# Attention with residual and layer norm over 32 batches: orders of their own for the first two and the last three batches

## The chip, the cores and the metric

The kernel runs on one NeuronCore of a Trainium2 chip. Its engines are TensorE (PE), VectorE (DVE), ScalarE (ACT), GpSimd (POOL) and SyncE (SP), which only issues DMAs here. The metric is the device time of one execution in microseconds (us), lower is better.

## The reference

For each of 32 batches: x is 256 rows of 384, adj is a 256 x 256 bias. Twelve heads of 32.

```python
q = (x @ Wq.T).reshape(B, N, 12, 32); k = (x @ Wk.T)...; v = (x @ Wv.T + bv)...
a = jnp.einsum('bnhd,bmhd->bhnm', q, k) * 384 ** -0.5 + adj[:, None]
pad_mask = jnp.all(a == 0, axis=-1)                    # such a row gives zero
a = nan_to_num(softmax(where(pad_mask[..., None], -inf, a)))
o = jnp.einsum('bhnm,bmhd->bnhd', a, v).reshape(B, N, 384) @ Wo.T + bo
out = layernorm(x + o)                                 # eps 1e-5, no scale
```

## The kernel before

Every engine has one program written out by hand, and only semaphores tie them together. A product in full precision is made of three: each operand is split into a high part (a rounding copy) and a low part (the difference), and PE multiplies high by high, high by low and low by high (`product`, line 534).

**Names.** The 384 columns are three groups of 128 (four heads each). `project_kq(t, name)` makes two of the six pieces of k and q of batch t: K01 in `bank_c`, K2Q0 and Q12 in `bank_b`, 18 products of 256 columns each. `save_kq` (ACT) copies the bank to `kq`, `split_kq` (POOL) makes `kq_hi` and `kq_lo`. `project_v(t, c)` makes half of v (9 products of 384 columns), `save_v` (DVE) adds the bias. `scores(t, g)` makes the scores of group g, 24 small products into the four banks `s_bank`. A unit u (0 to 11, four per group) is two heads for one half of the rows. `add_bias(t, u)` (DVE, line 784) adds adj and finds the maximum, `exps(t, u)` (ACT, line 439) takes the exponentials into `prob`, a ring of four.

**Two ways to turn the probabilities.** Groups 0 and 1: `square` (DVE, line 798) turns 32 x 32 squares into a staging area that lies in `w_f`, where the weights were loaded. When the four squares of a group stand, SP issues `store_squares` (to HBM) and, when that has landed, `load_squares` (back, blocks in the right partitions), each 1 MB. Group 2: `transposes` on PE into `bank_t`, `copy_probT` on ACT. Then `weigh(t, g)` (line 621) multiplies by v into `bank_a`, and `save_o` (ACT) copies.

**The end of a batch.** `invert` (DVE) and `widen_inv` (POOL) make the inverse sums, `spread` (PE, line 602) turns them into `bank_c`, `divide` (DVE) applies them; `split_o_hi` is ACT's, `split_o_lo` POOL's (line 346). `project_y(t, c)` multiplies by the output weights into `bank_b`; `residual` (DVE, line 872) adds x, to which POOL has added the bias (`add_bo`, which waits for the load `xr<-in_x`); `moments` (DVE), `deviation` (POOL), `normalise` (ACT), `store_out` (SP). `find_zero`, `flag` (PE, line 628), `read_flag` and `mask` (DVE) test once per batch whether a row of scores can be all zero; `mask` loads a register and branches over work that is not done here.

**Order.** Each engine has a function `step(t)` in which calls for batches t+2, t+1, t, t-1 and t-2 stand in a fixed order. `steps` runs it for t from -3 to 33, and calls for batches that don't exist are skipped (`alive`). So the first and the last batches run in the same order as the middle, with holes. Before a bank is written again PE waits until its reader is done (for instance `kq_saved`, `v_saved`, `y_saved` for `bank_b`). Before the first step, SP issues the loads of x, of k's weights in three pieces and of q's in one, and PE runs 24 warm-up products of 256 columns (`keep_warm`).

Of the kernel before, what the change touches and what calls it, by code (L numbers as in the profile page):

```python
# [3 lines left out]
F32 = mybir.dt.float32  # L4
# [3 lines left out]
ALU = mybir.AluOpType  # L8
# [5 lines left out]
P = 128  # L14
# [13 lines left out]
PROB_RING = 4  # L28
WARM_START = 24
DMA = 16  # L30
# [19 lines left out]
class Batch:  # L50


    def __init__(self, c):
        self.c, self.p = c, c % 2
        self.alive = 0 <= c < B
        self.first = c == 0
# [21 lines left out]


def steps(body):  # L80
    for c in range(-3, 34):
        body(Batch(c))


def build(nc, x, xT, adj, adjP, wqT, wkT, wvT, bv, woT, bo, out):
# [66 lines left out]

    W_Q, W_K, W_V, W_O = range(4)
    W_SPLIT = {W_Q: KC + 1, W_V: KC + 2, W_O: KC + 3}
# [3 lines left out]
    w_loaded = {w: sem(f"w_loaded_{name}") for w, name in ((W_Q, "q"), (W_V, "v"), (W_O, "o"))}  # L158
# [56 lines left out]
    with nc.Block() as block:  # L215

        @block.sync
        def _(sp):
# [38 lines left out]
            def store_out(t):  # L257
                sp.wait_ge(y_ready, t.count(NT, NT))
                sp.dma_start(out[t.c].rearrange("(c p) d -> p c d", p=P), y_out[:]).then_inc(stored, DMA)
# [10 lines left out]
            load_w(W_Q, wqT)  # L270
            load_bias_sq(Batch(0))
            load_xt(Batch(1))
            load_w(W_V, wvT)
            load_b(bv_all, bv)
            load_bias(Batch(0))
            load_b(bo_all, bo)
            load_w(W_O, woT)

            def step(t):
# [4 lines left out]
                if nxt.alive and not nxt.first:  # L284
                    load_bias(nxt)
                if t.alive:
                    store_squares(t, 0)
                if nxt3.alive and nxt3.c >= 2:
                    load_xt(nxt3)
                if t.alive:  # L290
                    load_squares(t, 0)
                    store_squares(t, 1)
                    load_xr(t)
                    load_squares(t, 1)
                if nxt2.alive and not nxt2.first:
                    load_bias_sq(nxt2)
                if prev2.alive:
                    store_out(prev2)

            steps(step)  # L300
            sp.wait_ge(stored, DMA * B)

        @block.gpsimd
        def _(pool):
# [69 lines left out]

            def step(t):
# [4 lines left out]
                if prev.alive:  # L380
                    widen_inv(prev)
                if nxt2.alive and not nxt2.first:
                    split_xt(nxt2)
                if nxt.alive:
                    split_kq(nxt, "K2Q0")
                    split_kq(nxt, "Q12")
                    split_kq(nxt, "K01")
# [578 lines left out]
```

## Time and profile before

| what | us |
|---|---|
| median of 3 runs | 763.73 |
| lowest and highest | 762.37 and 765.3 |
| the profiled execution | 762.95 |
| its span, first to last instruction | 761.0 |

The profiled execution took 1.95 us more than its span. All 22949 instructions are written out, none is looped. The mean granted clock of TensorE over the span is 0.978. Times in the rows below count from the start of the span.

### The profile page before, as it was taken

The numbers are of one execution on the slowest core, as the hardware profiler recorded it, in microseconds if no ns is written. First come the engines' busy times: TensorE is split into PE (matmuls) and PEld (weight loads), VectorE is DVE, ScalarE is ACT, GpSimd is POOL, SyncE is SP. The second block draws the span as 40 slices with busy tenths as digits, with TensorE's granted clock in tenths as the row PEclk, the third lists the DMA queues.
The fourth block names the chain that finished last, engine by engine and source line by source line (L and its number), as shares of the span: only waits on it lengthen the run. The fifth ranks groups of instructions, "written<-read, shape, count | busy, mean of one in ns | idle before, by whom it ended". The sixth has DMA issues, their size and how long they took to land.

```text
span 761.0 us, 22949 instructions
## 1 busy us (share of the span) xinstructions
PE 716.0 (94%) x7480; PEld 609.5 (80%) x7480; DVE 587.8 (77%) x2216; ACT 615.5 (81%) x1991; POOL 453.1 (60%) x518
## 2 busy tenths in 40 slices
PE   6889999999999999999999999999999999998753
PEld 5777888888888888888888888888888888886532
DVE  2677788888888888888888888888888888788821
ACT  2678888888988898888888988888889889888721
POOL 3345676766666676666666766666667666665331
PEclk7999999999999999999999999999999999999985
DMA  8087788888877877878778788777887887777631
GB/s 260 3 284 243 265 286 278 271 283 274 275 262 258 284 243 282 299 273 285 263 258 283 239 286 286 253 261 275 300 285 238 287 281 246 283 275 257 234 102 43
DMA packets 92664, 193.00 MB, mean 254 GB/s; under 512 B 4736, under 2 KB 51584, under 8 KB 84352
## 3 DMA queue, kind: packets, MB, share of 16 engines
q1 hardware_dynamic: 92544, 191.52, 74.7%
q8 instruction: 61, 1.00, 0.5%
q14 instruction: 59, 0.48, 0.2%
HBM read 111.80 MB, written 79.69 MB: 252 GB/s over the span
## 4 chain that ended last, share of the span: by engine, by line
PE 87%; DMA 3%; DVE 3%; POOL 2%; issue 2%; ACT 2%; SPq 0%; ACTq 0%; POOLq 0%; DVEq 0%
PE bank_b L534 45%; PE bank_a L621 12%; PE s_bank L580 11%; PE bank_t L591 9%; PE bank_c L534 9%; PE bank_c L602 2%; DVE neg L784 1%; DMA w_f<-in_wqT 1%; DMA xr<-in_x 1%; DMA sq_probT<-sq_dram 1%; POOL o_lo L346 1%; POOL kq_lo L336 1%; DMA sq_dram<-w_f 1%; ACT prob L439 1%; DVE w_f L798 0%
## 5 line engine op out<-in xcount | busy, mean ns | idle before, releaser
L439 ACT ACTIVATE prob<-neg,negmax 128x256 f32<-128x256 f32 x768 | 380.7, 501 | 40.8 <-DVE negmax L784 38.3
L784 DVE CUSTOM_DVE_ANT_0 neg<-s_bank,bias_sq 128x256 f32<-128x256 f32 x512 | 190.9, 410 | 48.9 <-PE s_bank L580 44.0
L798 DVE STREAM_TRANSPOSE w_f<-prob 128x512 f32<-128x512 f32 x256 | 173.1, 695 | 0.0
L439 ACT ACTIVATION_READ_ACCUMULATOR prob<-neg,negmax 128x1 f32 x768 | 147.9, 193 | 0.0
L336 POOL TENSOR_TENSOR kq_lo<-kq,kq_hi 128x512 fp32r<-128x512 f32 x96 | 124.2, 1293 | 7.7
L534 PE MATMUL bank_b<-xt_hi,w_hi 128*128 128x256 f32 x384 | 116.8, 304 | 7.1 <-DVE w_lo L760 3.3
L534 PE MATMUL bank_b<-xt_lo,w_hi 128*128 128x256 f32 x384 | 109.8, 286 | 0.0
L534 PE MATMUL bank_b<-xt_hi,w_lo 128*128 128x256 f32 x384 | 109.5, 285 | 0.0
L362 POOL TENSOR_SCALAR var_eps<-meanvar 128x2 f32<-128x2 f32 x32 | 7.3, 228 | 168.1 <-DVE meanvar L882 168.1
L784 DVE CUSTOM_DVE_ANT_0 neg<-s_bank,bias 128x256 f32<-128x256 f32 x256 | 92.3, 416 | 10.5 <-PE s_bank L580 10.5
L372 POOL TENSOR_TENSOR xr<-xr,bo_all 128x768 f32<-128x768 f32 x32 | 59.2, 1849 | 53.2 <-DMA xr<-in_x 53.1
L534 PEld LDWEIGHTS bank_b<-xt_hi,w_hi 128*128 128x128 f32 x384 | 74.3, 193 | 16.5 <-DVE w_lo L765 2.6
L591 PE MATMUL bank_t<-ident,prob 128*128 128x128 f32 x512 | 83.3, 285 | 2.2 <-ACT probT L449 2.1
L872 DVE TENSOR_TENSOR y<-bank_b,xr 128x384 f32<-128x384 f32 x64 | 35.7, 558 | 60.5 <-PE bank_b L534 60.3
L591 PEld LDWEIGHTS bank_t<-ident,prob 128*128 128x128 f32 x512 | 53.9, 141 | 33.1 <-issue 26.1
L534 PE MATMUL bank_b<-w_hi,o_hi 128*128 128x384 f32 x192 | 70.0, 365 | 10.7 <-POOL o_lo L346 9.8
L346 POOL TENSOR_TENSOR o_lo<-o_n,o_hi 128x512 fp32r<-128x512 f32 x64 | 63.9, 1020 | 24.8 <-ACT o_hi L464 24.7
L449 ACT ACTIVATE probT<-bank_t 128x512 f32<-128x512 f32 x128 | 75.0, 586 | 1.0 <-PE bank_t L591 1.0
L534 PEld LDWEIGHTS bank_b<-xt_lo,w_hi 128*128 128x128 f32 x384 | 74.8, 195 | 0.0
L534 PEld LDWEIGHTS bank_b<-xt_hi,w_lo 128*128 128x128 f32 x384 | 74.8, 195 | 0.0
L621 PE MATMUL bank_a<-sq_probT,v 128*32 128x256 f32 x1024 | 68.9, 386 | 2.5 <-DMA sq_probT<-sq_dram 2.4
L534 PE MATMUL bank_b<-w_hi,xt_hi 128*128 128x384 f32 x192 | 70.2, 366 | 0.7 <-ACT kq L422 0.7
(66 smaller groups left out, 1793.9 us busy)
## 6 DMA issues: line engine op xcount, KB each, us to landing
sq_dram<-w_f SPq DMA_DIRECT2D x64, 1024.0 KB, 6.4
sq_probT<-sq_dram SPq DMA_DIRECT2D x64, 1024.0 KB, 6.2
xt<-in_xT SPq DMA_DIRECT2D x32, 384.0 KB, 5.7
xr<-in_x SPq DMA_DIRECT2D x32, 384.0 KB, 6.1
out_y<-y_out SPq DMA_DIRECT2D x32, 384.0 KB, 6.4
bias_sq<-in_adjP SPq DMA_DIRECT2D x32, 256.0 KB, 6.4
bias<-in_adj SPq DMA_DIRECT2D x32, 256.0 KB, 6.9
w_f<-in_wkT SPq DMA_DIRECT2D x3, 192.0 KB, 4.3
```

Source lines behind the costliest of these rows:

```text
L336: nc.gpsimd.tensor_tensor(kq_lo[t.p][:, a:a + 2, :], kq[:, a:a + 2, :], kq_hi[t.p][:, a:a + 2, :].bitcast(F32), ALU.subtract).then_inc(kq_ ...
L346: nc.gpsimd.tensor_tensor(o_lo[:, a:b], o_n[:, a:b], o_hi[:, a:b].bitcast(F32), ALU.subtract).then_inc(o_ready, 1)
L372: nc.gpsimd.tensor_tensor(xr[t.p][:], xr[t.p][:], bo_all[:].unsqueeze(1).to_broadcast([P, NT, D]), ALU.add).then_inc(xr_ready, 1)
L439: nc.scalar.activation(prob[:, u % PROB_RING, k], neg[:, h, w.c], ACT.Exp, scale=-1.0, bias=negmax[t.p][:, w.c, h:h + 1], accum_out=sums[t ...
L449: nc.scalar.activation(probT[:, a:a + PAIR, :, P * w.c:P * (w.c + 1)], bank_t[:], ACT.Copy).then_inc(probT_act, 1)
L534: last = nc.tensor.matmul(ps, w_pair[a](k), m_pair[b](k), start=(k == 0 and e == 0), stop=(k == KC - 1 and e == 2))
L580: last = nc.tensor.matmul(s_bank[j][:, c, :], a[t.p][rows, KC + g, P * c:P * (c + 1)], b[t.p][rows, g, :], start=(e == 0), stop=(e == 2))
L591: last = nc.tensor.transpose(bank_t[:, k, m, :], prob[:, u % PROB_RING, k, P * m:P * (m + 1)], ident[:])
L621: last = nc.tensor.matmul(bank[f"PV{g}"][HD * j:HD * (j + 1), 0:N], v[t.p][:, m, HD * h:HD * (h + 1)], weights, start=(m == 0), stop=(m == ...
L784: nc.vector.tensor_tensor_reduce(out=neg[:, h, w.c], in0=s_bank[h % JH][:, w.c, :], in1=by[t.p][:, w.c, :], scale=-1.0, scalar=BIG, op0=AL ...
L798: nc.vector.transpose(sq_stage[w.g][:, :, a:a + PAIR, :, w.c].rearrange("p b h m s -> p (h m) b s"), prob[:, u % PROB_RING].rearrange("p k ...
L872: nc.vector.tensor_tensor(y[:, c, :], bank[f"Y{c}"][:, 0:D], xr[t.p][:, c, :], ALU.add).then_inc(y_saved, 1)
```

## The change

`steps` and `alive` are gone. Each engine has now three parts: `start()`, which covers what the old steps -3 to 1 did; `step(t)` for t from 2 to 28, word for word the old order; and `end()`, which covers the old steps 29 to 33. In `start` and `end` the calls stand in another order, written out for each engine. Further:

- q's weights are loaded, and split on ACT and DVE, in three pieces, as k's are.
- `scores` waits for K01 and K2Q0 with group 0 and for Q12 with group 1 only.
- For batch 31, spread, project_y, and weigh of groups 1 and 2 use banks of the scores and `bank_c` instead of the shared ones; before, these waited for the readers of the shared banks, and now for all of DVE's reductions.
- The low part of o of batch 31 is made on DVE.
- The last output is stored in two halves.
- The 24 warm-up products are of 128 columns; none are put between the first pieces (`FIRST_WARM` is 0, 0, 0).
- `w_hi` and `w_lo` of v and of the output weights move to other places in ACT's and DVE's lists, and squares of batch 0 wait for them, as they overwrite `w_f`.

```diff
-    W_SPLIT = {W_Q: KC + 1, W_V: KC + 2, W_O: KC + 3}
+    W_SPLIT = {W_K: 0, W_Q: KC, W_V: 2 * KC + 1, W_O: 2 * KC + 2}
...
+    last_bank = {"R0": s_flat[0], "Y0": s_flat[0], "R1": s_flat[1], "Y1": s_flat[1], "PV1": s_flat[2], "PV2": bank_c[:]}
+    def bank_at(t, name):
+        return last_bank[name] if t.last and name in last_bank else bank[name][:]
...
-            load_w(W_Q, wqT)
+            for k in range(KC):
+                sp.dma_start(w_f[:, W_Q, k], wqT[P * k:P * (k + 1), :]).then_inc(wq_loaded[k], DMA)
+            load_xt(Batch(1))
             load_bias_sq(Batch(0))
-            load_xt(Batch(1))
             load_w(W_V, wvT)
...
             def scores(t, g):
                 if g == 0:
                     pe.wait_ge(kq_ready["K01"], t.count(1, 1))
                     pe.wait_ge(kq_ready["K2Q0"], t.count(1, 1))
+                if g == 1:
                     pe.wait_ge(kq_ready["Q12"], t.count(1, 1))
...
         @block.tensor
...
+            def start():
...
+                project_kq(t0, "K01")
+                project_kq(t0, "K2Q0")
+                pe.wait_ge(kq_saved["K2Q0"], t0.count(1, 1))
+                project_kq(t0, "Q12")
+                scores(t0, 0)
+                pe.wait_ge(kq_saved["Q12"], t0.count(1, 1))
+                project_v(t0, 0)
+                pe.wait_ge(kq_saved["K01"], t0.count(1, 1))
+                project_kq(t1, "K01")
+                scores(t0, 1)
...
         @block.tensor
...
+            def end():
...
+                project_y(t30, 0)
+                copied(t31, 10)
+                transposes(t31, 11)
+                pe.wait_ge(neg_ready, t31.count(H * NT, H * NT))
+                weigh(t31, 1)
+                pe.wait_ge(neg_ready, t31.count(H * NT, H * NT))
+                spread(t31, 0)
+                pe.wait_ge(y_saved, t30.count(NT, 1))
+                project_y(t30, 1)
+                pe.wait_ge(o_n_ready, t30.count(2, 2))
+                weigh(t31, 2)
+                pe.wait_ge(neg_ready, t31.count(H * NT, H * NT))
+                spread(t31, 1)
+                pe.wait_ge(o_n_ready, t31.count(2, 1))
+                project_y(t31, 0)
+                pe.wait_ge(o_n_ready, t31.count(2, 2))
+                project_y(t31, 1)
...
         @block.gpsimd
...
+            def end():
...
+                add_bo(t29)
+                add_bo(t30)
+                split_o_lo(t30, 0)
+                split_o_lo(t30, 1)
+                deviation(t29)
+                widen_inv(t31)
+                add_bo(t31)
+                deviation(t30)
+                deviation(t31)
...
         @block.sync
...
+            def end():
...
+                store_squares(t31, 0)
+                store_out(t27)
+                load_squares(t31, 0)
+                store_squares(t31, 1)
+                store_out(t28)
+                load_squares(t31, 1)
+                load_xr(t31)
+                store_out(t29)
+                store_out(t30)
+                store_out(t31)
```

**Where instructions move.** First POOL at the start, from its first split on. Here `kq_hi0<-kq` is the split of a piece of batch 0, told apart by the semaphore it waits for, and `xt_hi1<-xt1` the split of x of batch 1. Before:

```order
L323 CAST xt_hi1<-xt1 128x768 [waits xt_ready,xt_loaded1]
L325 TENSOR_TENSOR xt_lo1<-xt1,xt_hi1 128x768 [waits xt_hi_ready]
L334 CAST kq_hi0<-kq 128x512 [waits kq_saved_K2Q0]
L336 TENSOR_TENSOR kq_lo0<-kq,kq_hi0 128x512 [waits kq_hi_ready_K2Q0]
L334 CAST kq_hi0<-kq 128x512 [waits kq_saved_Q12]
L336 TENSOR_TENSOR kq_lo0<-kq,kq_hi0 128x512 [waits kq_hi_ready_Q12]
L334 CAST kq_hi0<-kq 128x512 [waits kq_saved_K01]
L336 TENSOR_TENSOR kq_lo0<-kq,kq_hi0 128x512 [waits kq_hi_ready_K01]
```

and in the changed kernel:

```order
L398 CAST kq_hi0<-kq 128x512 [waits kq_saved_K01]
L400 TENSOR_TENSOR kq_lo0<-kq,kq_hi0 128x512 [waits kq_hi_ready_K01]
L398 CAST kq_hi0<-kq 128x512 [waits kq_saved_K2Q0]
L400 TENSOR_TENSOR kq_lo0<-kq,kq_hi0 128x512 [waits kq_hi_ready_K2Q0]
L387 CAST xt_hi1<-xt1 128x768 [waits xt_ready,xt_loaded1]
L389 TENSOR_TENSOR xt_lo1<-xt1,xt_hi1 128x768 [waits xt_hi_ready]
L398 CAST kq_hi0<-kq 128x512 [waits kq_saved_Q12]
L400 TENSOR_TENSOR kq_lo0<-kq,kq_hi0 128x512 [waits kq_hi_ready_Q12]
```

K01 moved from third to first, and x of batch 1 now stands behind K2Q0.

Second, DVE's last instructions, from the last reciprocal (`inv<-sums1`, batch 31) on. `y<-bank_b,xr0` is a residual of batch 30, `y<-...,xr1` of batch 31, `o_n` a division. Before:

```order
L853 RECIPROCAL inv<-sums1 128x24 [waits inv_wide_ready,prob_ready]
L872 TENSOR_TENSOR y<-bank_b,xr0 128x384 [waits y_ready,xr_ready,y_done]
L877 BN_STATS stats<-y 128x6 [waits y_saved]
L882 BN_AGGR meanvar<-stats 128x2 [waits bn_ready,rstd_ready]
L872 TENSOR_TENSOR y<-bank_b,xr0 128x384 [waits xr_ready,y_done]
L877 BN_STATS stats<-y 128x6 [waits y_saved]
L882 BN_AGGR meanvar<-stats 128x2 [waits bn_ready]
L862 TENSOR_TENSOR o_n<-o_raw1,bank_c 128x512 [waits o_ready,inv_spread,o_saved1,o_saved0]
L862 TENSOR_TENSOR o_n<-o_raw1,bank_c 128x256 [waits inv_spread,o_ready,o_saved2]
L872 TENSOR_TENSOR y<-bank_b,xr1 128x384 [waits y_ready,xr_ready,y_done]
```

and in the changed kernel:

```order
L1255 RECIPROCAL inv<-sums1 128x24 [waits inv_wide_ready,prob_ready]
L1283 TENSOR_TENSOR y<-bank_b,xr0 128x384 [waits y_ready,xr_ready,y_done]
L1288 BN_STATS stats<-y 128x6 [waits y_saved]
L1293 BN_AGGR meanvar<-stats 128x2 [waits bn_ready,rstd_ready]
L1264 TENSOR_TENSOR o_n<-o_raw1,s_bank0 128x512 [waits o_ready,inv_spread,o_saved1,o_saved0]
L1283 TENSOR_TENSOR y<-bank_b,xr0 128x384 [waits xr_ready,y_done]
L1288 BN_STATS stats<-y 128x6 [waits y_saved]
L1293 BN_AGGR meanvar<-stats 128x2 [waits bn_ready]
L1264 TENSOR_TENSOR o_n<-o_raw1,s_bank1 128x256 [waits inv_spread,o_ready,o_saved2]
L1274 TENSOR_TENSOR o_lo<-o_n,o_hi 128x512 [waits o_hi_ready,y_done]
L1274 TENSOR_TENSOR o_lo<-o_n,o_hi 128x256 [waits o_hi_ready]
L1283 TENSOR_TENSOR y<-s_bank0,xr1 128x384 [waits y_ready,xr_ready,y_done]
```

The division of batch 31 stands between the two residuals of batch 30 and reads `s_bank0` and `s_bank1`; the two low parts are new on DVE.

Third, SP at the start: q's weights (`w_f<-in_wqT`) and what stands around them. Before:

```order
L223 DMA xt0<-in_xT 128x3x256
L269 DMA w_f<-in_wkT 128x384 x3
L262 DMA w_f<-in_wqT 128x3x384
L232 DMA bias_sq0<-in_adjP 128x2x256
L223 DMA xt1<-in_xT 128x3x256
L262 DMA w_f<-in_wvT 128x3x384
```

and in the changed kernel:

```order
L228 DMA xt0<-in_xT 128x3x256
L280 DMA w_f<-in_wkT 128x384 x3
L282 DMA w_f<-in_wqT 128x384 x3
L228 DMA xt1<-in_xT 128x3x256
L237 DMA bias_sq0<-in_adjP 128x2x256
L273 DMA w_f<-in_wvT 128x3x384
```

One load of 128 x 3 x 384 became three of 128 x 384, and x of batch 1 moved ahead of the bias.

## Rows read from the trace of the kernel before

**Rows 1.** The page's first part: busy us (share of the span) xinstructions.

```profile
PE 716.0 (94%) x7480; PEld 609.5 (80%) x7480; DVE 587.8 (77%) x2216; ACT 615.5 (81%) x1991; POOL 453.1 (60%) x518
```

**Rows 2.** Windows: stretch, length, busy by engine, PE's clock, DMA share, GB/s.

```profile
73.30:95.60 22.30, 22.07 (x238) 18.76 (x234) 18.38 (x70) 18.25 (x61) 14.38 (x17) 1.00 0.73 251
95.60:117.45 21.85, 21.85 (x238) 18.72 (x234) 18.07 (x70) 19.00 (x64) 14.98 (x17) 1.00 0.82 278
663.95:761.00 97.05, 67.34 (x634) 54.18 (x630) 56.46 (x204) 57.11 (x183) 39.12 (x52) 0.88 0.52 186
```

**Rows 3.** Groups by form in 109.3 to 131.2: busy us, mean ns | idle before.

```profile
L784 DVE CUSTOM_DVE_ANT_0 neg<-s_bank,bias_sq 128x256 f32<-128x256 f32 x16 | 6.0, 411 | 1.6 <-PE s_bank L580 1.6
L798 DVE STREAM_TRANSPOSE w_f<-prob 128x512 f32<-128x512 f32 x8 | 5.4, 696 | 0.0
```

**Rows 4.** Chain that ended last, 0 to 70: start us, us, what.

```profile
11.30 1.37 DVE w_lo L765
...
15.05 0.61 ACT kq L422
...
15.70 4.21 PE bank_b L534 x18
...
24.52 1.28 POOL kq_lo L336
...
25.84 0.98 PE s_bank L580 x24
26.82 2.35 PE bank_b L534 x18
...
38.02 4.71 DMA sq_dram<-w_f
...
42.82 5.94 DMA sq_probT<-sq_dram
```

**Rows 5.** Timeline of PE at 9.7: start us, us, instruction, [idle before].

```profile
9.74 0.39 PE L534 MATMUL bank_b<-xt_hi,w_hi 128*128 128x256 f32 x1 [1.92 <-DVE w_lo L760]
```

**Rows 6.** Windows of the fill; the clock is the third number from the end.

```profile
10.40:12.70 2.30, 0.00 (x0) 0.00 (x0) 1.36 (x1) 0.87 (x1) 0.67 (x1) 0.54 0.99 320
15.00:20.70 5.70, 5.01 (x24) 5.00 (x24) 0.00 (x0) 1.20 (x2) 2.14 (x3) 0.50 0.60 212
20.70:25.00 4.30, 3.98 (x33) 3.77 (x31) 0.35 (x1) 2.44 (x3) 3.00 (x4) 0.98 0.02 4
```

**Rows 7.** Timeline of DVE, 24 to 50.

```profile
24.65 2.35 DVE L765 SCALAR_TENSOR_TENSOR w_lo<-w_f,w_hi 128x1152 fp32r<-128x1152 f32 x1 [11.98 <-ACT w_hi L406]
...
32.21 1.35 DVE L765 SCALAR_TENSOR_TENSOR w_lo<-w_f,w_hi 128x1152 fp32r<-128x1152 f32 x1
...
46.41 0.42 DVE L784 CUSTOM_DVE_ANT_0 neg<-s_bank,bias_sq 128x256 f32<-128x256 f32 x1 [1.85 <-ACT prob L439]
```

**Rows 8.** Timeline of SP: issues of stores and loads of squares.

```profile
43.30 1.34 SPq L245 DMA_DIRECT2D sq_dram<-w_f  x1
...
51.35 0.36 SPq L254 DMA_DIRECT2D sq_probT<-sq_dram  x1
...
716.01 0.33 SPq L245 DMA_DIRECT2D sq_dram<-w_f  x1
...
725.47 0.36 SPq L254 DMA_DIRECT2D sq_probT<-sq_dram  x1
```

**Rows 9.** Chain that ended last, 690 to 761.

```profile
719.42 6.91 DMA xr<-in_x
...
733.53 1.41 PE bank_a L621 x16
...
737.05 1.80 PE bank_b L534 x9
...
750.15 3.26 PE bank_b L534 x9
...
753.44 0.57 DVE y L872
```

More of the change, by code:

```diff
@@ L379, in step @@
                 prev2 = t.later(-2)
[L380 to L387, printed above, removed]
-                if prev2.alive:
-                    deviation(prev2)
-                if t.alive:
-                    add_bo(t)
-                if prev.alive:
-                    split_o_lo(prev, 0)
-                    split_o_lo(prev, 1)
@@ L530, in _ @@
+            start()
+            for c in range(2, 29):
+                step(Batch(c))
+            end()
         @block.tensor
@@ L748, in _ @@
-            steps(step)
+                copied(prev, 10)
+                transposes(prev, 11)
+                pe.wait_ge(v_saved, t.count(NT, 1))
+                project_v(t, 1)
+                pe.wait_ge(o_n_ready, prev2.count(2, 2))
+                project_kq(nxt, "K01")
+                pe.wait_ge(v_saved, t.count(NT, 2))
+                project_y(prev2, 0)
+                pe.wait_ge(o_saved[0], prev.count(1, 1))
+                weigh(prev, 1)
+                scores(t, 2)
+                pe.wait_ge(y_saved, prev2.count(NT, 1))
@@ new lines, in step @@
+                project_kq(nxt2, "K2Q0")
+                pe.wait_ge(o_saved[1], prev.count(1, 1))
+                weigh(prev, 2)
+                copied(prev, 11)
+                transposes(t, 8)
+                pe.wait_ge(kq_saved["K2Q0"], nxt2.count(1, 1))
+                project_y(prev2, 1)
+                pe.wait_ge(kq_saved["K01"], nxt.count(1, 1))
+                spread(prev, 0)
+                pe.wait_ge(o_saved[2], prev.count(1, 1))
+                flag(t)
+                copied(t, 8)
@@ new lines, in step @@
+                transposes(t, 9)
+                scores(nxt, 0)
+                pe.wait_ge(y_saved, prev2.count(NT, 2))
+                project_kq(nxt2, "Q12")
+                pe.wait_ge(flag_read, t.count(1, 1))
+                weigh(t, 0)
+                copied(t, 9)
+                transposes(t, 10)
+                pe.wait_ge(o_n_ready, prev.count(2, 1))
+                spread(prev, 1)
+                pe.wait_ge(kq_saved["Q12"], nxt2.count(1, 1))
+                project_v(nxt, 0)
@@ L750, in _ @@
+            start()
+            for c in range(2, 29):
+                step(Batch(c))
+            end()
         @block.vector
@@ L935, in step @@
-                if prev.alive:
-                    divide(prev, 1)
-            steps(step)
+                add_bias(t, 3)
+                square(t, 0)
+                save_v(t, 0)
+                square(t, 1)
+                add_bias(t, 4)
+                square(t, 2)
+                add_bias(t, 5)
+                save_v(t, 1)
+                invert(prev)
+                add_bias(t, 6)
+                square(t, 3)
+                add_bias(t, 7)
+                residual(prev2, 0)
@@ L941 @@
+            start()
+            for c in range(2, 29):
+                step(Batch(c))
+            end()
 _INS = ["x", "xT", "adj", "adjP", "wqT", "wkT", "wvT", "bv", "woT", "bo"]
```

946 lines of the change are left out of this document (705 added, 241 removed).

## The prediction

> **What bounds the kernel now.** Read the page's line of engines first [rows 1]: TensorE (PE) is busy for 94% of the span. Then the windows cut where PE enters a step [rows 2]. A step of the middle takes 21.85 us and PE is busy for all of it, VectorE (DVE) for 18.07 and ScalarE (ACT) for 19.00. From PE's entry into step 3 (95.60) to that into step 29 (663.95) are 26 steps in 568.35 us, 21.86 each. So PE bounds the middle, and 32 batches at that pace are 699.2 us. The span is 761.0: 61.8 us lie in filling and draining. The stretch before step 2 ends at 73.30, and the one from step 29 is 97.05 long with PE busy for 67.34, part of that at half clock [rows 2]. The change rewrites these two stretches; the 27 steps between keep their order. So the sum has three terms: when PE enters step 2, the middle, and what follows PE's entry into step 29.
>
> **The middle.** Now 22.30 for step 2, then 568.35 [rows 2]. The finer waits of scores change nothing here: in a step K01 is the last of the three that POOL splits, before and after. Step 2's extra 0.45 is a first-time wait, since the low part of o for batch 0 comes late; I let it go and take 21.85 + 568.35 = 590.2.
>
> **The fill.** Prices of the work: a unit of scores on DVE is two reductions of 411 ns that overlap, about 0.69; a square 0.65, by 696 ns that overlap likewise [rows 3]. POOL splits one half of q and k in 0.6 + 1.28, ACT copies it in 0.61 [rows 4].
>
> Before, PE gets the last third of k's weights at 9.74 [rows 5]. Then q's weights come as one piece whose low part is ready at 12.67 (11.30 + 1.37). PE starts again there and does 18 products in 4.21 us, against 2.35 at full clock. The order K2Q0, Q12, K01 lets POOL end with K01 at 25.80, and scores wait for all three: 25.84 [rows 4].
>
> After: at 9.74 PE has 12 products of K01 left that need k's weights alone. They cover q's split by thirds (each a third of 1.37 on DVE, 0.46, and as much on ACT: ready by some 11.5, if the loads keep their pace). The clock is low from 10.4 to 20.7 and full after, having come back 5.0 us into the unbroken work that starts at 15.70 [rows 6]. The new work is unbroken from 9.74, so I let it come back at 14.7: K01 ends at 12.0 and K2Q0 at 15.5 (0.234 a product cold by the row of 4.21, 0.13 warm by that of 2.35). ACT: 16.1. POOL, done with K01 by then: 18.1. First scores at 18.2, 7.6 us earlier.
>
> From here DVE leads. It must first do v's low part, 1.35 alone and 2.35 beside a busy POOL [rows 7]; POOL is busy, and ACT's high part comes first (about 1), so it is done at 19.4. Four units: 22.2. PE meanwhile does v, K01 of batch 1 and the second scores, to 24.2. DVE then has 8 units (5.5), 6 squares (3.9), a copy of v (0.5, an estimate from its width), the output weights' low part (1.35 to 2.35) and the zero test (0.2): 11.5 to 12.5, and with 0.3 of waiting the last square of batch 0 stands at 37.0.
>
> That square must go to HBM and back before PE weighs group 1. From issue of the store to issue of the load it took 51.35 - 43.30 = 8.05 and 725.47 - 716.01 = 9.46 [rows 8], since the load of group 0 was under way; the first store, alone, took 4.71 and its load 5.94 [rows 4]. So a round is 10.7 undisturbed and 14.0 to 15.4 in company. I take 14.2, near the disturbed ones, since group 0's load overlaps here too: 51.2. PE is there at 47 and waits. Then weighing and scores, 1.9 (53.1); after them PE's own queue (spread, K2Q0 and Q12 of batch 3, weighing, transposes: 6.8) leads to the flag at 59.9. The flag and its branch cost DVE about 2 (the idle 1.85 before 46.41) [rows 7], four units 2.8, scores 0.9: PE enters step 2 at **65.5**, against 73.3. Bounds: 62.5 with rounds undisturbed, 67.5 with 15.4 and a late split of v.
>
> The 24 warm-up products are halved in columns. They run while PE waits for data anyway: nothing, but for the clock (below).
>
> **The drain.** Count from PE's entry into step 29 (663.95). DVE's list up to the last square of batch 31 is two steps of 18.07 busy plus 1.85 of branch (39.8), five more units (3.5), eight squares (5.2), and v and reciprocal (1.3): 49.8; that DVE runs some 2 ahead of PE I set against its waits. Before, the store of these squares was issued at 716.01 [rows 8], 52.1 on this count. So they gain 2.3 only. A round of 14.2 lands them at 64.0. Before, PE weighs them at 733.53 [rows 9], 69.6: ahead of it in PE's queue stands the first half of project_y of batch 30. That waits for POOL's low part of o, and POOL stands at add_bo of batch 31, whose input is issued at 719.42 and lands 6.91 later. In the new order the projection still stands ahead, but POOL splits o of batch 30 before add_bo of batch 31, and group 1 has a bank of its own. So PE weighs as the squares land: gain 5.6.
>
> From there to the end, before: 761.0 - 733.5 = 27.5, with the second half of Y of batch 30, its moments and normalisation in line, POOL's low part of o, and two projections cold, 3.26 each [rows 9]. After: weigh 1.0, spread 0.4, that half of Y 1.8, weigh 1.0, spread 0.2 (4.4); save, divide, high part and low part, the last on DVE, about 0.4 each with their hops (1.9); two projections at full clock, 1.80 each as at 737.05 (3.5); then residual, moments, POOL's chain, normalisation and store as at present, 761.0 - 753.44 = 7.6. Sum 17.4. Storing by halves gives little, both wait for one deviation. So 64.0 + 17.4 = **81.4**, against 97.05. Bounds: 77, if rounds are undisturbed, and DVE's own list (3 x 19.9, and the moments and divisions added at the end) leads; 86, if the rounds of both groups are long and the last projections stay cold (2 x 1.46).
>
> Sum: 65.5 + 590.2 + 81.4 = 737.1 of span. The profiled execution took 762.95 for a span of 761.0, so 739.0; it lies 0.8 below the median of the runs shown. Forecast **739.0**.
>
> **Clock.** Where the granted clock is low, PE had been idle for most of the time before [rows 6]. The Trainium skill, "TensorE: Matmul & The Clock Gate", section "What's actually happening", says that throttled is the default and activity releases it. This speaks against halving the warm-up; by it the fill would be that of rival 1.
>
> **DVE beside POOL.** The same split took 2.35 and 1.35 [rows 7]. The Trainium skill, "SBUF — State Buffer", section "Who interferes with whom", says that a VectorE instruction with two SBUF inputs contends with GpSimd reads. By it both splits in the new fill cost the longer time, and the fill ends near 66.
>
> **Rivals.**
> 1. Cold start: PE stays at half clock through K01, K2Q0 and Q12 of batch 0. By the rows of 4.21 and 2.35 that is 1.86 more per 18 products, 5 for all, less what is counted: 3 more, of which POOL's splitting hides one. About 741. For it: half the warm-up, no fillers between chunks. Against: unbroken work from 9.74. Chance 0.12.
> 2. Rounds undisturbed, so that DVE's list sets both ends: 62.5 + 590.2 + 77, near 732. For it: SP's new order moves other loads off these stores. Against: 716.01 meets the load of the group before, and that pair is the same. Chance 0.13.
> 3. The squares of batches 30 and 31 queue behind one another, each round 15.4 or more, paid twice: 4 to 7 more, 743 to 746. Chance 0.13.
> 4. One end doesn't pay. A residual waits for the normalisation of the batch before (there is one y), and the drain loses most of its gain: 753. Chance 0.04.
> 5. Slower. PE enters the middle at another offset to DVE and SP, and in each step a load of squares lands after PE wants it. The gain is gone once a step loses 24.0/27 = 0.9; at 1.2 the time is 771. For it: the wait on that load is what I see in the fill. Against: the steps take 21.85 whatever the fill did, and ACT leaves 2.85 a step. Chance 0.02.
> 6. The finer waits do nothing, as in the middle. But then POOL's Q12 would be late in batch 0 by 4.5, and the time 743; the order K01, K2Q0 speaks against it. Chance 0.02.
>
> **How the numbers follow.** Forecast 0.54. The range takes in 1, 2 and most of 3, and the bounds of both ends: 731 to 747. A measurement tells about 0.5% (3.8 us) from no change: faster 0.97, same 0.01, slower 0.02.
>
> **What would show it.** Right: first scores near 18, steps of 21.85, PE waiting for the load of group 1 in batches 0 and 31, full clock in the last projections, an end 81 after step 29 begins. Wrong: another pace in the middle, first scores after 20, or PE in the drain waiting mostly for DVE or POOL.

## The result, and the profile after

| what | before, us | after, us |
|---|---|---|
| median, lowest to highest, beside each other | 763.24 (762.37 to 765.3) | 737.65 (735.0 to 742.57) |
| ratio, with its 95% interval | | 0.967 (0.961 to 0.972) |
| the profiled execution and its span | 762.95, 761.0 | 737.71, 735.9 |

The forecast was 739.0. The profiled execution is cut at the same places as in the prediction, PE's entry into step 2 and into step 29. Each cut is the first `transposes` of unit 11 of the batch before. The span is the sum of the three stretches:

| | before | forecast | after |
|---|---|---|---|
| PE enters step 2 | 73.3 | 65.5 | 64.26 |
| middle | 590.65 | 590.2 | 593.79 |
| from PE's entry into step 29 | 97.05 | 81.4 | 77.82 |
| span | 761.0 | 737.1 | 735.9 |

So the forecast of the time is close because three misses cancel, which is luck: 1.2 too much in the fill, 3.6 too little in the middle, 3.6 too much in the drain. First the page's line of engines, which answers [rows 1], and the windows of [rows 2]: steps 2 and 3, then step 11, which turned out to matter, then the drain. Columns: stretch, length, busy by engine, PE's clock, DMA share, GB/s.

```profile
PE 709.5 (96%) x7480; PEld 605.0 (82%) x7480; DVE 590.1 (80%) x2220; ACT 616.6 (84%) x1993; POOL 453.1 (62%) x516
```

```profile
64.26:86.84 22.58, 21.92 (x238) 18.80 (x234) 18.25 (x71) 19.13 (x65) 14.21 (x16) 1.00 0.76 252
86.84:108.68 21.84, 21.84 (x237) 18.71 (x233) 18.06 (x70) 18.98 (x64) 14.23 (x16) 1.00 0.78 270
261.60:284.74 23.14, 22.15 (x237) 18.85 (x233) 18.26 (x70) 19.92 (x65) 14.12 (x16) 1.00 0.76 257
658.04:735.90 77.86, 63.15 (x634) 50.83 (x630) 58.22 (x206) 57.32 (x182) 38.36 (x50) 0.95 0.66 235
```

The busy times of the other engines have hardly moved, and PE's fell by 6.5. So most of the 25.1 us that the span lost was idle time of PE. In the drain its busy time went from 67.34 in [rows 2] to 63.15 with the granted clock up from 0.88 to 0.95, and the rest of that stretch's 19.2 us is waiting that is gone. Step 3 takes 21.84 as it did, but step 11 takes 23.14 with PE idle for 1 us.

**The fill.** The chain that ended last, up to POOL's split of K2Q0, which answers [rows 4] and [rows 5], and then the first scores, from PE's timeline:

```profile
2.21 4.95 DMA w_f<-in_wkT
...
7.73 0.57 DVE w_lo L1162
...
8.35 2.94 PE bank_c L779 x12
11.29 0.02 issue
11.31 1.11 ACT kq L532
...
13.28 1.11 POOL kq_lo L400
...
14.51 0.61 POOL kq_hi L398
...
15.21 1.29 POOL kq_lo L400
```

```profile
16.74 0.39 PE L828 MATMUL s_bank<-kq_hi 32*128 32x256 f32 x4
```

PE starts the last 12 products of K01 at 8.35, not at 9.74 as in [rows 5]. They are still at half clock (2.94 / 12 = 0.245 each). The windows of this profile print a clock of 1.00 here, but its first record of the clock is at 11.8; what shows the lower level is that the products start 0.21 apart, and 0.12 apart from 11.72 on. POOL then splits K01 and K2Q0 one behind the other, and the first scores start at 16.74 in place of 25.84.

**The drain.** PE's waits of over half a microsecond from its entry into step 29, from the timeline; the number in brackets is the idle time ahead of the instruction, with what ended it:

```profile
670.27 0.39 PE L828 MATMUL s_bank<-kq_hi 32*128 32x256 f32 x4 [0.61 <-POOL kq_lo L400]
...
701.58 1.09 PE L850 MATMUL bank_c<-ident,inv_wide 128*128 128x128 f32 x4 [3.07 <-POOL inv_wide L418]
...
713.11 0.66 PE L839 MATMUL bank_t<-ident,prob 128*128 128x128 f32 x4 [0.54 <-ACT probT L563]
...
719.08 1.07 PE L869 MATMUL s_bank<-sq_probT,v 128*32 128x256 f32 x16 [1.71 <-DMA sq_probT<-sq_dram]
...
725.34 0.42 PE L779 MATMUL s_bank<-w_hi,o_hi 128*128 128x384 f32 x1 [1.64 <-DVE o_lo L1274]
```

The chain around the last squares of batch 31, which answers [rows 8] and [rows 9]:

```profile
706.94 0.71 DVE w_f L1200
...
707.73 5.78 DMA sq_dram<-w_f
...
713.59 5.36 DMA sq_probT<-sq_dram
718.95 0.14 issue
719.08 1.07 PE s_bank L869 x16
720.15 0.58 PE s_bank L850 x4
```

Store and load follow each other with nothing between. PE weighs 0.13 after the landing, and 16.8 later the span ends (27.5 before). The chain of that tail does not go through PE's wait of 1.64 but through the normalisation of batch 30:

```profile
726.09 1.32 ACT y_out L584 x2
...
727.53 0.57 DVE y L1283
```

The first residual of batch 31 waits for that normalisation, since there is one `y`; PE's product for it was done at 727.16. PE's last product ends at 728.75, and the second residual starts at 728.95. So two paths end within 0.2 to 0.4 us of each other, and a gain on one of them alone would have been worth no more.

### The profile page after: what moved, and what is told of

The parts are those of the page before. It is cut to its first block, busy times and chain, and to the rows that moved or that the text cites. A ratio compares the mean times of both kernels' runs of the same rounds, so it can differ in the third digit from the quotient of the medians.

```text
span 735.9 us, 22957 instructions
## 1 busy us (share of the span) xinstructions
PE 709.5 (96%) x7480; PEld 605.0 (82%) x7480; DVE 590.1 (80%) x2220; ACT 616.6 (84%) x1993; POOL 453.1 (62%) x516
## 4 chain that ended last, share of the span: by engine, by line
PE 81%; DMA 8%; POOL 4%; DVE 3%; issue 2%; ACT 1%; SPq 0%; DVEq 0%; POOLq 0%; ACTq 0%
PE bank_b L779 40%; PE bank_a L869 11%; PE s_bank L828 10%; PE bank_c L779 8%; PE bank_t L839 8%; DMA sq_dram<-w_f 3%; DMA sq_probT<-sq_dram 3%; PE bank_c L850 2%; DMA xr<-in_x 2%; POOL kq_lo L400 1%; DVE neg L1183 1%; DVE w_f L1200 1%; DMA w_f<-in_wkT 1%; POOL xt_lo L389 1%; POOL xt_hi L387 0%
## 5 line engine op out<-in xcount | busy, mean ns | idle before, releaser
L779 PE MATMUL bank_b<-xt_hi,w_hi 128*128 128x256 f32 x384 | 115.2, 300 | 1.4 <-POOL xt_lo L389 0.7
L1183 DVE CUSTOM_DVE_ANT_0 neg<-s_bank,bias 128x256 f32<-128x256 f32 x256 | 92.5, 415 | 10.3 <-PE s_bank L828 10.3
L410 POOL TENSOR_TENSOR o_lo<-o_n,o_hi 128x512 fp32r<-128x512 f32 (+1 forms) x62 | 62.0, 1022 | 34.0 <-ACT o_hi L578 33.5
L398 POOL CAST kq_hi<-kq 128x512 fp32r<-128x512 f32 x96 | 58.9, 613 | 25.1 <-ACT kq L532 10.9
L779 PE MATMUL bank_b<-w_hi,o_hi 128*128 128x384 f32 x186 | 66.3, 356 | 0.3 <-POOL o_lo L410 0.2
```

What stands on the lines that cost most here:

```text
L398: nc.gpsimd.tensor_copy(kq_hi[t.p][:, a:a + 2, :], kq[:, a:a + 2, :]).then_inc(kq_hi_ready[name], 1)
L410: nc.gpsimd.tensor_tensor(o_lo[:, a:b], o_n[:, a:b], o_hi[:, a:b].bitcast(F32), ALU.subtract).then_inc(o_ready, 1)
L779: last = nc.tensor.matmul(ps, w_pair[a](k), m_pair[b](k), start=(k == 0 and e == 0), stop=(k == KC - 1 and e == 2))
L1183: nc.vector.tensor_tensor_reduce(out=neg[:, h, w.c], in0=s_bank[h % JH][:, w.c, :], in1=by[t.p][:, w.c, :], scale=-1.0, scalar=BIG, op0=AL ...
```

## The experiments

Executions of one kernel differ by several microseconds (735.0 to 742.57 above), so a kernel with one execution only is judged by the cuts and waits of its trace, not by its time. The cuts scatter too. In the eight profiles that have the new start with 24 warm-up products, PE enters step 2 at 63.2 to 64.8. In the nine whose start and steps are those of the changed kernel, warm-up aside, the middle is 591.8 to 594.2. In the eight that have its drain, the drain is 77.8 to 81.2, and the profile of after is the shortest of them. Only the tail from the last squares on is steady: 16.77 to 16.81 in nine of the ten profiles that keep it, the tenth being run 10.

**1 and 2. One end alone.** `fill_only` has the new start, weights by chunk and finer waits, with the old order for steps 29 to 33; `drain_only` the reverse.

```diff
 # fill_only: on every engine
             for c in range(2, 29):
                 step(Batch(c))
-            end()
+            for c in range(29, 34):
+                old_step(Batch(c))
```

```diff
 # drain_only: on every engine; scores wait finely from batch 29 on only
+            for c in range(-3, 29):
+                step(Batch(c))
+            end()
-            steps(step)
```

> The new start, with q's weights by thirds and the finer waits, and the old order, banks and single store at the end (steps 29 to 33 as before). Theory (fill, middle and drain are three terms that add up): PE enters step 2 near 64.3 as in the changed kernel, the drain from step 29 takes 97 as before, and the time is 763.2 less 9 for the fill, plus what the middle loses: 754 to 758. Rival (the new start only pays because the new end takes up its offset): above 760.

> The old start, old steps to 28, then the new end with its banks, its low part on DVE and the stores by halves; the finer waits of scores are used for batches 29 to 31 alone, where the new order needs them. Theory: PE enters step 2 at 73.3, a step is 21.85, the drain takes 78, and the time is near 763.2 - 19 = 744. If the middle's loss of the changed kernel comes from the offset that the new start leaves, it is absent here: 743 to 745, and 746 to 748 if it comes in any run. Rival (terms don't add): above 750.

| | time, us | ratio to before | step 2 | middle | from step 29 |
|---|---|---|---|---|---|
| fill_only | 756.3 (754.07 to 757.68) | 0.991 (0.988 to 0.993) | 64.76 | 592.73 | 97.79 |
| drain_only | 745.28 (743.4 to 746.58) | 0.977 (0.974 to 0.979) | 72.20 | 591.89 | 79.28 |

Against 763.39 beside them that is 7.1 and 18.1, in sum 25.2; both ends together gave 25.6. The ends add up, neither takes from the other. `fill_only` is where it was expected, `drain_only` 0.3 above the 743 to 745 that were to hold if the middle lost nothing. The middle is 1.2 to 2.1 longer than in the profile of before in both. `drain_only` runs the code of before up to step 28, so its 1.2, and its 72.20 at step 2 in place of 73.3, are scatter between executions and no effect of the change.

**3. Finer waits undone.** In the changed kernel, scores of group 0 wait for all three of POOL's splits again, up to batch 28.

```diff
-                if g == 1:
+                if g == (0 if t.c <= 28 else 1):
                     pe.wait_ge(kq_ready["Q12"], t.count(1, 1))
```

> The changed kernel with scores of group 0 waiting for all three of POOL's splits again, up to batch 28. By rival 6 of the prediction the finer waits do nothing: first scores at 16.7, step 2 at 64.3, time as the changed kernel's. By my reckoning POOL splits Q12 behind K2Q0, 1.9 more: first scores 18.6 to 19, step 2 1.9 to 4.5 later, time 739 to 742; the middle is unchanged.

750.21 in one execution, span 748.4: step 2 at 74.11, 9.9 later than with finer waits, and later even than before the whole change. The middle is 594.89, the drain 79.36. First PE's wait, from the timeline of this kernel, then POOL's timeline at the same place:

```profile
22.26 0.59 PE L828 MATMUL s_bank<-kq_hi 32*128 32x256 f32 x4 [5.51 <-POOL kq_lo L400]
...
46.59 0.59 PE L828 MATMUL s_bank<-kq_hi 32*128 32x256 f32 x4 [2.84 <-POOL kq_lo L400]
```

```profile
15.15 1.29 POOL L400 TENSOR_TENSOR kq_lo<-kq,kq_hi 128x512 fp32r<-128x512 f32 x1
16.39 1.95 POOL L387 CAST xt_hi<-xt 128x768 fp32r<-128x768 f32 x1
18.42 1.80 POOL L389 TENSOR_TENSOR xt_lo<-xt,xt_hi 128x768 fp32r<-128x768 f32 x1
20.16 0.61 POOL L398 CAST kq_hi<-kq 128x512 fp32r<-128x512 f32 x1
20.86 1.26 POOL L400 TENSOR_TENSOR kq_lo<-kq,kq_hi 128x512 fp32r<-128x512 f32 x1
```

K01 and K2Q0 are there at 16.4. Between them and Q12, POOL's list has the split of x of batch 1, 3.8 us. I had counted Q12's own 1.9 and overlooked what stands ahead of it in POOL's queue, so both the 1.9 to 4.5 of the expectation and the 4.5 of rival 6 were too small. Beside the 5.5 and 2.8 us of waiting, the first products behind each wait run at half clock (0.59 against 0.39 for the same four). So the whole gain of the fill hangs on the finer waits together with the new order. The middle is 1.1 longer than in after, with 4.2 of waits for squares by name (2.5 in after); no wait for POOL's splits stands in it, as forecast.

**4 and 5. More warm-up.** `warm_48` has 48 warm-up products in place of 24; `warm_fill` has 48 and fillers between the chunks of the first weights.

```diff
-WARM_START = 24
+WARM_START = 48
-FIRST_WARM = (0, 0, 0)
+FIRST_WARM = (8, 8, 12)    # warm_fill only
```

> The changed kernel with 48 warm-up products of 128 columns instead of 24, as many columns as before the change, nothing between the first pieces. The trace of the changed kernel shows products of K01 at 0.21 each up to 11 us. Theory: with the longer warm-up the clock is full when the first k chunk comes, K01 ends some 2 earlier, near 9, and the first scores start near 15.5 instead of 16.7; but DVE and ACT lead from there, so PE enters step 2 at 63.5 to 64.3. Rival (the clock sets the fill): step 2 a full 2 us earlier, near 62. If the warm-up is still running when the chunk comes, the start is later by that.

> As the run before, and 8, 8 and 12 more warm-up products before the three first pieces of K01. Theory: the clock stays full through K01 and K2Q0, first scores at 15 to 15.5, and step 2 is entered at 63.5 to 64.3, since the work that follows is DVE's. Rival (the clock sets the fill): near 62.

`warm_48` runs K01 at full clock. The chain of this kernel:

```profile
7.85 1.72 PE bank_c L779 x12
...
13.49 2.44 POOL kq_lo L400
...
16.07 0.98 PE s_bank L828 x21
```

12 products take 1.72 in place of 2.94, but scores start only 0.7 earlier, since POOL's next split takes 2.44 instead of 1.29 beside DVE's split of v's weights. (That is no effect of the warm-up: it takes 2.44 in `after_again` too, whose first scores come at 16.65.) PE is in step 2 at 62.62, and the span is 735.9 as in after (738.33 in one execution; `warm_fill`: step 2 at 63.53, span 735.2, 737.05). The expectation had 63.5 to 64.3 if DVE leads and 62 if the clock sets the fill; `warm_48` lies nearer the second, `warm_fill` at the edge of the first. The three profiles with 48 warm-up products (`bias_late_warm` below has 63.09) enter step 2 at 62.6 to 63.5, those with 24 at 63.2 to 64.8. So the halved warm-up costs some 0.8 at step 2 by the medians, which is within the scatter, and nothing that a time shows. The clock behaves as the Trainium skill, "TensorE: Matmul & The Clock Gate", section "What's actually happening", says: activity releases it. The trace agrees: behind 48 warm-up products K01 runs at 0.143 a product, behind 24 at 0.245.

**6. The wait of 3.07 taken away.** PE's longest wait in the drain is for `inv_wide` of batch 30, which stands on POOL behind a low part of o of batch 29. `spread_free` moves it and DVE's `invert` and `divide` ahead.

```diff
 # gpsimd, end()
-                split_o_lo(t29, 0)
                 widen_inv(t30)
+                split_o_lo(t29, 0)
 # vector, end()
                 save_v(t31, 0)
+                invert(t30)
                 square(t31, 0)
+                divide(t29, 1)
                 square(t31, 1)
                 square(t31, 2)
                 square(t31, 3)
-                invert(t30)
                 add_bias(t31, 4)
-                divide(t29, 1)
```

> The changed kernel, but in the drain the reciprocal of batch 30 and the second division of batch 29 stand before the squares of batch 31 in DVE's list, and POOL widens the inverses of batch 30 before the low part of o of batch 29. Aim: the 3.07 us for which PE waits before the spread of batch 30. Theory (that wait lies on the way to the last squares, by v's second half, and PE then waits 1.71 for them): the wait shrinks to under 1, the last square comes 1 to 2 earlier, the drain from step 29 is 1 to 2 shorter than 77.8. Rival (DVE's list sets the last square): the wait moves, the last store is issued at the same distance from step 29 within 0.5, the drain is 77.5 to 78.

Measured 736.08, span 734.2, from step 29 78.53 (77.82 in after). The wait is gone, and another stands in its place:

```profile
701.11 1.92 PE L869 MATMUL bank_a<-sq_probT,v 128*32 128x256 f32 x16 [4.29 <-DMA sq_probT<-sq_dram]
...
717.47 1.07 PE L869 MATMUL s_bank<-sq_probT,v 128*32 128x256 f32 x16 [0.97 <-DMA sq_probT<-sq_dram]
```

PE now waits for the squares of batch 30, which land no earlier: 45.3 after step 29, 44.4 in after, where they landed 0.2 before PE wanted them. So the 3.07 was time that PE had anyway until these squares landed, and costs nothing that is seen: a wait's length is not its price. The last store is issued 51.1 after step 29 (49.7 in after), which is neither the theory's gain nor within the 0.5 of the rival; the drain is inside the scatter.

**7. The last square before the copy of v.** `square_first` squares unit 7 of batch 31 ahead of `save_v`.

```diff
-                save_v(t31, 1)
                 square(t31, 7)
+                save_v(t31, 1)
```

> The changed kernel, but DVE makes the last square of batch 31 before it saves v's second half, for which it idled 0.92 us. Theory (the round trip of the last squares is the next bound): the store is issued 1.4 earlier counted from step 29, PE weighs group 1 about 1.2 earlier, and the drain ends 1.0 to 1.4 earlier, near 76.6. Rival (another wait is as late, the low part or the residual's wait for the normalisation of batch 30): weighing is earlier, the end within 0.3 of 77.8.

737.5, span 735.6. The store is issued 50.0 after step 29 (49.7 in after), and lands 6.5 later; from step 29 78.88. No gain is to be seen, though DVE's part came out: counted from the store of group 0 the last store is issued 7.2 later, against 8.0 in after. It then meets 3.5 us of the load of group 0 instead of 2.7, and takes 6.47 instead of 5.78. So what the move gained until the issue, the transfer lost again, as far as one profile of each shows.

**8. Shared banks at the end.** Batch 31 uses the old banks, with the old waits.

```diff
-        return last_bank[name] if t.last and name in last_bank else bank[name][:]
+        return bank[name][:]
```

> The changed kernel with batch 31 back in the shared banks, with the waits on their readers: weighing group 1 and 2 wait for the copies of the group before, spreads for the divisions, the projections for the residuals; the order is the same. Theory (what the banks are worth): group 1 still waits for its load; the second spread, which waits for the first division, and weighing group 2, which waits for the copy of group 1, are late by 0.5 each, and the second projection waits 0.65 for the residual of the first: drain 1 to 2 longer, near 79.5. Rival (the banks carry the drain's gain): 5 longer or more.

738.37, span 736.5. The squares are weighed 61.3 after step 29 (61.0 in after). From there to the end it takes 17.85 in place of 16.8, by one new wait, of the last projection for the residual that reads the one `bank_b`:

```profile
727.72 0.44 PE L779 MATMUL bank_b<-w_hi,o_hi 128*128 128x384 f32 x1 [0.97 <-DVE y L1283]
```

So the banks of scores are worth 1.1 here, well clear of the 0.04 by which this tail scatters, and the drain of 79.14 is near the 79.5 expected. Most of what `end()` gains is not its banks but its order, with the low part on DVE that run 9 prices.

**9. The last low part on POOL.**

```diff
 # vector, end()
-                split_o_lo(t31, 0)
-                split_o_lo(t31, 1)
 # gpsimd, end()
                 deviation(t30)
+                split_o_lo(t31, 0)
+                split_o_lo(t31, 1)
```

> The changed kernel with the low part of o of batch 31 on POOL, behind its deviation of batch 30. Theory: 2.0 us on POOL in place of 1.1 on DVE, and the deviation of batch 30 (1.9) stands ahead of it: the last projections start 1.5 to 3 later, and if PE's idle time reaches that of before the change they run at half clock, 1.45 more each. Drain 79.5 to 83. Rival (hidden, since the residual of batch 31 waits for the normalisation of batch 30 anyway): under 78.3.

739.34, span 737.5, drain 82.17, inside the expected 79.5 to 83. From the last squares to the end 21.4 in place of 16.8, the largest single effect found in the drain:

```profile
724.67 0.66 PE L781 MATMUL s_bank<-w_hi,o_hi 128*128 128x384 f32 x1 [4.02 <-POOL o_lo L410]
```

Both halves go through POOL in 1.91 by the chain, behind the deviation of batch 30. PE waits 4.02 in place of 1.64, and then its last 18 products take 5.84 at the lower clock, by the chain, against 3.41. That is 2.4 by the wait and 2.4 by the clock, less the 0.2 by which PE was ahead of DVE in after.

**10. The changed kernel again.**

> The changed kernel once more, unchanged, beside the three that follow. 735 to 742 as in its own comparison. If the 3 us that the middle has too much are the company of the stores, the middle is again 592 to 594.5 and steps over 21.95 are again those in which the load of squares lands 0.1 to 0.3 us before PE weighs it. If that was one unlucky execution, the middle is 590.5 and the slow steps are gone.

737.08 (734.93 to 739.43), ratio 0.964 (0.960 to 0.967). The middle is 593.75 again, and the steps over 22.1 are 2, 11, 12, 18 and 20 (in after 2, 11, 12, 13, 14 and 28). PE's named waits in the middle, from the table of waits (total, times, longest), of before, of after and of this run:

```profile
PE bank_b L534 <- issue: 0.2, 1, 0.2
```

```profile
PE bank_a L869 <- DMA sq_probT<-sq_dram: 2.5, 4, 1.0
PE bank_b L779 <- POOL o_lo L410: 0.2, 1, 0.2
```

```profile
PE bank_a L869 <- DMA sq_probT<-sq_dram: 3.3, 4, 1.4
```

Of the 3.1 us by which both middles are longer than that of before, 2.5 and 3.3 are waits for the load of squares by name. The waits stand in steps 2, 11, 13 and 28 of after and in 2, 11, 18 and 20 of this run. In the drain this execution had a last round of 13.1 us, store 7.06 and load 6.04, where after had 11.2; its store was issued 7.0 after that of group 0 and met 3.4 us of group 0's load. The wait and the window behind it:

```profile
718.69 1.32 PE L869 MATMUL s_bank<-sq_probT,v 128*32 128x256 f32 x16 [3.85 <-DMA sq_probT<-sq_dram]
```

```profile
719.00:724.00 5.00, 5.00 (x41) 3.85 (x37) 1.17 (x2) 1.35 (x3) 1.81 (x1) 0.66 0.09 33
```

After 3.85 us idle the granted clock falls to 0.66 in that stretch, mostly the lower of its two levels, and squares to end takes 18.35 in place of 16.8. In after the wait was 1.71 and the clock stayed. So a long round is paid twice.

**11 and 12. The squares' store with less ahead of it.** In step 11 of after, SP issues the output (384 KB) at 262.1 and the bias of the next batch (256 KB) at 262.6. Both take 8.4 to 8.5 to land, and the first store of squares is issued at 266.09 into that. The chain there, and the wait at its end, from the timeline:

```profile
266.09 7.48 DMA sq_dram<-w_f
...
273.64 6.66 DMA sq_probT<-sq_dram
```

```profile
280.44 1.07 PE L869 MATMUL bank_a<-sq_probT,v 128*32 128x256 f32 x16 [0.97 <-DMA sq_probT<-sq_dram]
```

In most steps this store takes 4.7 to 5.5, and the load lands 1 to 2.5 ahead of PE. PE was ready to weigh 13.4 after the issue of the store (280.44 - 0.97 - 266.09); store and load took 14.1. `bias_late` issues the bias behind the second store; nobody reads it before the next step. `bias_late_warm` has 48 warm-up products besides.

```diff
-                load_bias(nxt)
                 store_squares(t, 0)
                 load_xt(nxt3)
                 load_squares(t, 0)
                 store_squares(t, 1)
+                load_bias(nxt)
```

> In the 27 steps SP issues the bias of the next batch (256 KB) behind the second store of squares, no longer ahead of the first. Theory: the first store of squares takes 4.7 us where bias and output have landed before it is issued, and up to 7.5 where they still run; a quarter of a megabyte less ahead of it is about 1 us (256 KB at the 265 GB/s of that stretch). Stores of group 0 then stay at 5 to 6, the load lands 0.5 us or more ahead of PE, the middle falls to 590.5 to 592, and the time by 1.5 to 3, to 734 to 736. Rival a: the bias only moves into the company of the second store and its load, whose slack is 0.4 to 0.7 at its smallest: the middle stays at 593 or grows to 595. Rival b: the slow steps have another cause (PE's own list at that point): no change.

> bias_late with 48 warm-up products in place of 24. Alone, the 48 brought PE into step 2 1.6 us earlier and left the span where it was. If the company of the stores took that gain back, this kernel keeps it: 1 to 1.6 below bias_late. If an earlier fill is eaten by something else (the drain's last round), it is equal to bias_late.

| | time, us | ratio to before | step 2 | middle | from step 29 |
|---|---|---|---|---|---|
| after_again | 737.08 (734.93 to 739.43) | 0.964 (0.960 to 0.967) | 63.25 | 593.75 | 80.04 |
| bias_late | 739.2 (735.77 to 740.25) | 0.967 (0.963 to 0.970) | 63.82 | 592.85 | 80.15 |
| bias_late_warm | 739.36 (738.33 to 740.56) | 0.968 (0.965 to 0.971) | 63.09 | 592.20 | 81.19 |

The store issued at 266 in step 11, from the lines of its source line, after and then `bias_late` (min, median, max):

```profile
DMA to landing us min/median/max: 7.5/7.5/7.5
```

```profile
DMA to landing us min/median/max: 5.2/5.2/5.2
```

And PE's named waits in the middle of `bias_late`:

```profile
PE bank_a L869 <- DMA sq_probT<-sq_dram: 1.0, 1, 1.0
PE bank_c L850 <- DVE o_n L1264: 0.6, 3, 0.2
```

The mechanism holds: with a quarter of a megabyte less ahead, the store is 2.3 shorter, steps 11 to 14 are back at 21.9, and PE waits for squares once, for 1.0, in step 2. Step 11 takes 22.2 to 23.3 in ten of the twelve profiles with the bias ahead, and 21.85 in both with it behind. The time doesn't follow. Other steps (5, 15, 20, 24, 26) take 22.1 to 22.3, the middle is only 0.9 shorter, which is inside its scatter, and the drain is no shorter. The expected 734 to 736 was missed, and `bias_late_warm` didn't keep its earlier start. None of the tries beats the changed kernel.

## Why the prediction came out as it did

**Fill, 65.5 against 64.26.** The mechanism is right: finer waits and the order K01, K2Q0, Q12 bring the first scores forward. Terms that were mis-sized:
- The first scores were due at 18.2 and came at 16.74. The last third of k's weights was ready 1.4 earlier (8.35), which I had left at the 9.74 of [rows 5]. It landed at 6.3 to 7.6 in the twelve profiles with the new loads, at 7.7 and 8.5 in the two with the old; q's load in thirds behind it may be why, but that wasn't tried alone. The clock came back at 11.7, three products into K2Q0, not at 14.7: the 18 products of K2Q0 stand between 11.08 and 13.71, 0.146 each. I had counted from 9.74, as from the 15.70 of [rows 4] to the 20.70 of [rows 6]. PE had by then been at work since 6.49, with one pause of 0.21, and before the change too it had worked from 12.72 with one pause of 0.69 ahead of 15.70, which I had left out.
- DVE's list took 20.0 from there, not 18.8. The last square was stored at 36.77, against the 37.0 forecast: the two misses cancel.
- The round: 14.2 forecast, 10.3 measured (4.9 for the store, 5.3 for the load). I took the disturbed rows since the load of group 0 was to overlap. That step failed in its size: before, the store of group 1 was issued 5.3 after that of group 0 (43.30 - 38.02) and met 5.5 us of its load; after, it was issued 8.6 later and met 2.3 us:

```profile
28.14 0.34 SPq L250 DMA_DIRECT2D sq_dram<-w_f  x1
...
33.16 0.37 SPq L259 DMA_DIRECT2D sq_probT<-sq_dram  x1
...
36.77 0.34 SPq L250 DMA_DIRECT2D sq_dram<-w_f  x1
```

  The load issued at 33.16 took 5.9. So the bound of 10.7 was the right value, and the wait of 4 us for this load, which I had named as a sign, never came: PE weighs at 48.43 without waiting.
- From there to step 2 it took 15.8, not 14.3.

**Middle, 590.2 against 593.79.** Here a statement failed, "the steps take 21.85 whatever the fill did". PE waits for squares in some steps, 2.5 us by name, since the slack of that load is small in the worst steps: in before it lands 0.41 ahead of PE in step 3 and 0.42 in step 11, in most steps 1 us or more. It is the mechanism of rival 5, which I had priced only as an all-or-nothing loss of 0.9 in each step. I should have read the least slack of the load over all steps of before, not the length of the steps. That the new ends are its cause isn't shown: one execution of before was profiled, its middle of 590.65 is the shortest of all profiles here, and `drain_only`, which runs the same code up to step 28, has 591.89 with a step 11 of 22.48.

**Drain, 81.4 against 77.82.** The last square was to be stored 49.8 after the entry, and was at 49.7. From the weighing to the end 17.4 was forecast and 16.8 measured, with both last projections at full clock. But the sum of 17.4 followed PE and DVE's low part, and the chain that led went through the normalisation of batch 30, which rival 4 names; the two paths end nearly together, so that the sum came out is in part luck. 3.0 of the 3.6 are again the round: 14.2 against 11.2, and 13.1 in the second profile of the same kernel. Here too the stores stand further apart (8.0 us, 4.7 before) and less of the load of group 0 is met (2.7 us, 5.5 before). The rounds at the ends of all kernels with the new orders took 10.2 to 13.2, so the choice near the disturbed end was wrong. And the size of the miss is that of one profile: the same drain took up to 81.2 in others.

**The rivals.** Cold start (1): part of it, half clock in K01 and three products more; the runs with 48 warm-up products price it at some 0.8 in the fill and nothing in the time. Rounds undisturbed (2): this is nearly what happened at both ends; with the forecast middle the span would be 64.26 + 590.2 + 77.82 = 732.3. Squares queueing (3): not seen in after; in `after_again` the last round lost 1.9 and the cold tail 1.6. One end doesn't pay (4): excluded by runs 1 and 2. Slower by late squares (5): real in the middle, with some 3 us lost of the 24 that it needed. Finer waits do nothing (6): wrong; without them the fill is 9.9 longer, where I had put 4.5.

**What stays open.** In the ten profiles with new fill and new drain, PE enters step 29 between 655.3 and 658.0 and weighs the last squares between 716.0 and 720.0, and the second doesn't follow the first (716.0 and 719.7 from entries at 655.3, 719.1 from 658.0). Something other than PE's position sets when the last store is issued; DVE's waits in the drain go to several things (up to 3.3 for v), and no single run isolates it. How long the store then takes goes with how much of the load of group 0 it meets (last section), but no run changes that alone. Not tried alone either: q's weights in thirds, and the last output in two halves.

## What to carry to other kernels

A coarse wait costs nothing where its last part comes last anyway. When an order is changed, look at what the producer's queue has between the part that is needed and the part that is waited for: here 3.8 us of other work, and 9.9 us at the entry to the middle. When two transfers are taken to disturb each other, work out from the new order how much of them still overlaps. For a transfer that a compute engine waits for, read its least slack over all repetitions, and price a wait that you remove by what lands next, not by its length. In a drain, a wait of nearly 4 us on PE cost its own length and the clock behind it, and waits of up to 1.8 only their length.

## What the runs showed of the hardware

- DVE's split of v's weights (128 x 1152, 1.35 us alone) and POOL's work beside it: the one that starts first keeps its time and the other pays. In seven of the 14 profiles POOL's subtraction starts first, by 0.03 to 0.23 us: it takes 1.3, and DVE 2.3 to 2.5. In the other seven DVE starts first, by 0.03 to 0.05: it takes 1.36, and POOL 2.4. Both orders occur in the same kernel (after and `after_again`). [rows 7] had shown only DVE's side. The Trainium skill, "SBUF — State Buffer", section "Who interferes with whom", names the shared read interface of the two for such instructions and says that issue order decides who blocks; these traces agree.
- 1 MB stored by SP took 4.7 to 5.5 us in most steps, with x of a later batch (384 KB) issued 0.4 behind it, and up to 7.5 with 640 KB issued 4 us ahead and not landed. At batch 29, where nothing is issued behind it until it has landed, it took 3.9 to 4.9 in the 14 profiles, 4.1 in the median, so what is issued behind seems to cost something too.
- The store of group 1 beside the load of group 0, 1 MB each, at batches 0 and 31 of all 14 profiles: where at most 2.4 us of the load were left, the store took 4.4 to 5.6 (18 cases); with 2.7 left 5.8 (one); with 3.4 to 3.7 left 6.0 to 7.1 (five); with 5.4 to 6.3 left 7.9 to 10.1 (four). Other transfers ran beside some of them, and no run changes the overlap alone.
